# A flamingo block on one core: variance, root and split move to GpSimd, the first norm is joined by bn_aggr, y gets three buffers

## The reference, cut to what matters

```python
x = x + tanh(g_x) * ((ctx @ Wv) @ Wout + bout)         # n_kv == n_q here: one key per query
h = layernorm(layernorm(x), ln1_g, ln1_b)              # width 256
h = bitlinear(h, w1, b1)                               # 1024 wide
h = layernorm(gelu(h), ln2_g, ln2_b)
x = x + tanh(g_f) * bitlinear(h, w2, b2)               # back to 256
# bitlinear: rows scaled by 127 / max|row| and rounded, weights rounded to -1, 0, 1
```

## Time and profile before

| | us |
|---|---|
| median of 3 runs (lowest, highest) | 402.39 (400.57, 402.53) |
| the profiled execution, its own time | 400.17 |
| its span, first to last instruction | 398.4 |
| busy over the span: DVE, PE, ACT, POOL | 330.2, 304.1, 277.9, 220.9 |
| mean granted TensorE clock, share of full | 0.949 |

### The profile page before, as it was taken

How to read it: one execution, slowest core, us unless ns; L and a number is a source line. 1 busy time by engine, 2 the same in 40 slices (tenths; PEclk the granted TensorE clock), 3 DMA queues, 4 the chain that set the end, 5 groups by cost and what they waited for, 6 DMA issues and landing times. The chain is left out here.

```text
span 398.4 us, 5821 instructions
## 1 busy us (share of the span) xinstructions
PE 304.1 (76%) x1690; PEld 187.9 (47%) x1690; DVE 330.2 (83%) x794; ACT 277.9 (70%) x446; POOL 220.9 (55%) x118
## 2 busy tenths in 40 slices
PE   2887295868888888888888888888888766758364
PEld 2776153434646464646464646464646342414043
DVE  0389366888999999999999999999999995957782
ACT  1314447678697979797979797979797968678431
POOL 4021444829484848484848484848485858454600
PEclk9999689989999999999999999999999996969669
DMA  7665404119183828383838383838270707062635
GB/s 226 244 225 181 132 0 130 56 53 185 54 186 107 190 102 182 108 183 110 184 107 184 108 183 109 180 111 172 67 170 18 170 17 160 26 115 71 135 77 160
DMA packets 97686, 51.56 MB, mean 129 GB/s; under 512 B 86535, under 2 KB 88768, under 8 KB 97654
## 3 DMA queue, kind: packets, MB, share of 16 engines
q1 hardware_dynamic: 96758, 51.14, 50.7%
q10 hardware_dynamic: 896, 0.04, 0.1%
HBM read 21.78 MB, written 8.41 MB: 76 GB/s over the span
## 5 line engine op out<-in xcount | busy, mean ns | idle before, releaser
L337 POOL TENSOR_TENSOR y<-u,g_bc 128x1024 f32<-128x1024 f32 x64 | 150.3, 2368 | 62.5 <-DVE parts L594 49.7
L694 DVE TENSOR_TENSOR y<-y,slot_c 128x1024 f32<-128x1024 f32 x64 | 77.7, 1214 | 9.9 <-PE slot_c L965 9.8
L698 DVE TENSOR_REDUCE amax<-y 128x1 f32<-128x1024 f32 x64 | 78.1, 1220 | 2.2
L432 ACT ACTIVATE q<-y,s 128x1024 f16<-128x1024 f32 x64 | 69.8, 1139 | 11.5 <-DVE s L725 11.5
L459 ACT ACTIVATE junk<-u,usum 128x1024 bf16<-128x1024 f32 x64 | 73.5, 1149 | 2.1
L1003 PE MATMUL bank_f<-w2T,q2T 128*128 128x256 f16 x512 | 66.1, 276 | 2.6 <-DVE res L745 2.4
L320 POOL TENSOR_TENSOR rstd<-var,half_neg 128x8 f32<-128x8 f32 x18 | 29.5, 1641 | 69.0 <-DVE var L645 56.6
L965 PE MATMUL slot_c<-ln_rows,rows 128*128 128x512 bf16 x128 | 41.3, 406 | 30.8 <-DVE y L694 16.3
L944 PE MATMUL bank_q<-wvo,ctxT 128*128 128x256 f32 x232 | 59.7, 387 | 0.0
L1003 PEld LDWEIGHTS bank_f<-w2T,q2T 128*128 128x128 f16 x512 | 50.2, 99 | 14.6 <-DVE res L745 4.8
L423 ACT ACTIVATE q<-h,s 128x256 f16<-128x256 f32 x64 | 27.3, 496 | 32.7 <-DVE s L685 32.7
(11 more groups left out here) (114 smaller groups left out, 426.8 us busy)
## 6 DMA issues: line engine op xcount, KB each, us to landing
c_in<-in_ctx SPq DMA_DIRECT2D x16, 512.0 KB, 3.4
x_in<-in_x SPq DMA_DIRECT2D x16, 512.0 KB, 4.1
out<-res SPq DMA_DIRECT2D x32, 256.0 KB, 2.8
y<-in_L_ffn_w SPq DMA_DIRECT2D x2, 1024.0 KB, 9.3
u<-in_L_xattn_Wkv SPq DMA_DIRECT2D x1, 1024.0 KB, 6.8
u<-in_L_xattn_Wout SPq DMA_DIRECT2D x1, 1024.0 KB, 10.0
q2T<-q SPq DMA_TRANSPOSE x64, 3.3
g_bc<-in_L_ffn_ln_g SPq DMA_DIRECT2D x1, 512.0 KB, 4.5
```

The costliest lines, as they stand in the source:

```text
L337: nc.gpsimd.tensor_tensor(y[:, k % 2, t, :], u[:, t, :], g2_bc[:, :], ALU.mult).then_inc(gain2_done, 1)
L432: nc.scalar.activation(q2[:, t, :], y[:, k % 2, t, :], ACT.Copy, scale=s2[:, t:t + 1]).then_inc(q2_done, 1)
L694: nc.vector.tensor_tensor(line, line, slot_c[:, :], ALU.add).then_inc(y_done, 1)
L698: nc.vector.tensor_reduce(amax2[:, t:t + 1], y[:, k % 2, t, :], AX.X, ALU.max, apply_absolute_value=True).then_inc(amax2_done, 1)
```

## The change: what it does

`variance`, `deviations` and `split` run on POOL, as does the new `norm_first`, which turns the first norm's mean and variance into the statistics' form. On DVE four `bn_aggr` replace the seven instructions of `join`, and stand behind the first `row`. `first` and `second` become one `scales` of six instructions over both norms at once. y has three buffers, `rows` two. From stage 3 on attention goes to `slot_a` after its last gelu, both halves at the end of PE's body. `quantise` of t = 2 and 3 moves behind the squares, its transposes (`turn_second`) to the next body of SP, behind a store, and its second product to the next body of PE, between corrections. There is one body more (S + 2). ACT takes the rows ahead of the quantising.

The diff, cut to its core (the renamed buffers and their indices are left out):

```diff
             for i in bodies:
+                if live(i - 3):
+                    store(i - 3, 0)
+                    turn_second(i - 3, 2)
+                    turn_second(i - 3, 3)
                 if live(i):
                     turn_first(i)
-                if live(i - 2):
-                    for t in range(T):
-                        turn_second(i - 2, t)
-                if live(i - 3):
-                    store(i - 3, 0)
-                    store(i - 3, 1)
                 if live(i + 4) and i + 4 > 1:
                     load_x(i + 4)
                 if live(i + 5) and i + 5 > 1:
                     load_context(i + 5)
-            store(S - 1, 0)
-            store(S - 1, 1)
+                if live(i - 2):
+                    turn_second(i - 2, 0)
+                    turn_second(i - 2, 1)
+                if live(i - 3):
+                    store(i - 3, 1)
...
-                    wait(pool, q2_done, T * (k - 2) + t + 1)
+                    wait(pool, q2_done, T * (k - 3) + t + 1)
                     wait(pool, gelu_done, T * k + t + 1)
-                    nc.gpsimd.tensor_tensor(y[:, k % 2, t, :], u[:, t, :], g2_bc[:, :],
+                    nc.gpsimd.tensor_tensor(y[:, k % 3, t, :], u[:, t, :], g2_bc[:, :],
                                             ALU.mult).then_inc(gain2_done, 1)
...
+                def norm_first(k):
+                    wait(pool, moments_done, k + 1)
+                    wait(pool, std_done, k)
+                    wait(pool, split_steps, split_count(k - 2))
+                    nc.gpsimd.tensor_scalar(stat[:, 0, :], moments[:, :, 0], -1.0, None, ALU.mult)
+                    nc.gpsimd.tensor_scalar(var[:, 0, :], moments[:, :, 1], 1.0 + LN_EPS,
+                                            LN_EPS * LN_EPS, ALU.mult, ALU.add) \
+                        .then_inc(var1_done, 1)
+                def variance(k):
+                    wait(pool, square_done, T * k + T)
+                    wait(pool, std_done, i + 2)
+                    wait(pool, split_steps, split_count(i))
+                    nc.gpsimd.tensor_scalar(stat[:, 2, :], usum[:, :], -1.0 / H, None, ALU.mult)
+                    nc.gpsimd.tensor_scalar(var[:, 1, :], usq[:, :], 1.0 / float(H) ** 3, LN_EPS,
+                                            ALU.mult, ALU.add).then_inc(var2_done, 1)
+                def deviations():
+                    wait(pool, rstd_done, i + 2)
+                    wait(pool, split_steps, split_count(i - 1))
+                    nc.gpsimd.tensor_tensor(stat[:, 1:4:2, :], var[:, :, :], rstd[:, i % 2, :, :],
+                                            ALU.mult).then_inc(std_done, 1)
+                def split(n):
+                    shape = [P, T, KINDS, NPART]
+                    if n == 0:
+                        wait(pool, std_done, min(i + 2, S + 2))
+                        wait(pool, var1_done, min(i + 2, S))
+                        wait(pool, var2_done, min(i, S))
+                        wait(pool, scales_ready, scales_after(i - 1))
+                        wait(pool, rows_done, i + 1)
+                    else:
+                        wait(pool, split_steps, split_count(i - 1) + n)
+                    if n % 2 == 0:
+                        value = (stat_t, rest[:, :, :], rest[:, :, :])[n // 2]
+                        op = nc.gpsimd.tensor_copy(
+                            parts_q[:, :, :, 3 * (n // 2):3 * (n // 2) + 3],
+                            value.unsqueeze(3).to_broadcast(shape))
+                    else:
+                        value = (stat_t, rest[:, :, :])[n // 2]
+                        op = nc.gpsimd.tensor_tensor(rest[:, :, :], value,
+                                                     parts_q[:, :, :, 3 * (n // 2)], ALU.subtract)
+                    op.then_inc(split_steps, 1)
                 if -1 <= i <= S:
-                    wait(pool, split_steps, split_count(i))
+                    deviations()
+                if -1 <= i <= S + 1:
+                    for n in range(5):
...
+                    norm_first(0)
+                if i == -1:
+                    norm_first(1)
                 if i == 0:
                     pool.wait_ge(g2_in, 16)
                 if live(i - 1):
-                    if i > 1:
-                        gain(i - 1, 2)
                     gain(i - 1, 3)
                 if live(i + 1) and i > -1:
                     gain_first(i + 1)
+                if live(i + 2) and i > 0:
+                    norm_first(i + 2)
                 if live(i):
                     gain(i, 0)
                     gain(i, 1)
+                    gain(i, 2)
                 if i == 0:
-                    gain(0, 2)
+                    norm_first(2)
+                if live(i):
+                    variance(i)
                 if -1 <= i + 1 <= S:
                     root(i + 1)
...
-                    wait(act, second_ready, second_count(k, t // 2))
+                    wait(act, scales_ready, k + 3 + (t // 2 if k == S - 1 else 0))
                     wait(act, q2T_in[t], 16 * k)
-                    nc.scalar.activation(q2[:, t, :], y[:, k % 2, t, :], ACT.Copy,
-                                         scale=s2[:, t:t + 1]).then_inc(q2_done, 1)
+                    nc.scalar.activation(q2[:, t, :], y[:, k % 3, t, :], ACT.Copy,
+                                         scale=scale[:, (k + 1) % 2, 1, t:t + 1]).then_inc(q2_done, 1)
                 def take_rows():
                     wait(act, rows_done, i + 2)
-                    wait(act, shift1_done, min(i + 1, S))
-                    wait(act, corr_done, T * (i - 1))
-                    wait(act, hid_done, T * min(i, S))
-                    wait(act, ffn_done, T * (i - 2))
-                    nc.scalar.copy(rows[:, :, :].rearrange("p a n -> p (a n)"),
+                    wait(act, shift1_done, min(i, S))
+                    wait(act, corr_done, T * (i - 2))
+                    wait(act, hid_done, T * (i - 1))
+                    wait(act, ffn_done, T * (i - 3))
+                    nc.scalar.copy(rows[:, i % 2, :, :].rearrange("p a n -> p (a n)"),
                                    slot_c[:, 0:P].bitcast(BF16)).then_inc(rows_copied, 1)
...
+                if 0 < i <= S:
+                    take_rows()
+                if live(i + 3) and i > 0:
+                    take_context(i + 3, 0)
                 if live(i - 2):
                     quantise(i - 2, 0)
                     quantise(i - 2, 1)
-                if 0 < i <= S:
-                    take_rows()
+                if live(i + 3) and i > 0:
+                    take_context(i + 3, 1)
+                if live(i):
+                    for t in range(T):
+                        gelu(t)
+                        square(t)
                 if live(i - 2):
                     quantise(i - 2, 2)
                     quantise(i - 2, 3)
                 if i == S + 1:
                     take_rows()
-                if live(i):
-                    gelu(0)
-                    square(0)
-                if live(i + 3) and i > 0:
-                    take_context(i + 3, 0)
-                if live(i):
-                    gelu(1)
-                    square(1)
-                    gelu(2)
-                    square(2)
                 if i == 0:
                     take_context(3, 0)
-                if live(i):
-                    gelu(3)
-                    square(3)
-                if live(i + 3) and i > -3:
-                    take_context(i + 3, 1)
+                    take_context(3, 1)
...
+                def join(k):
+                    wait(dve, bn_done, k + 1)
+                    wait(dve, var1_done, k)
+                    for t in range(T):
+                        op = nc.vector.bn_aggr(moments[:, t, :], bn[:, t, :])
+                    op.then_inc(moments_done, 1)
...
+                def scales(kinds=slice(0, 2), those=slice(0, T)):
+                    shape = [P, kinds.stop - kinds.start, those.stop - those.start]
+                    base = 3 * (i + 1 + (those.start > 0))
+                    one = (slice(None), kinds, those)
+                    power = rstd[:, i % 2, kinds, those]
+                    if kinds.start == 0:
+                        wait(dve, amax1_done, i + 2)
+                    wait(dve, amax2_done, T * (i - 1) + those.stop)
+                    wait(dve, rstd_done, i + 2)
                     wait(dve, split_steps, split_count(i))
-                    nc.vector.tensor_scalar(stat[:, 2, :], usum[:, :], -1.0 / H, None, ALU.mult)
-                    nc.vector.tensor_scalar(var[:, 1, :], usq[:, :], 1.0 / float(H) ** 3, LN_EPS,
-                                            ALU.mult, ALU.add).then_inc(var2_done, 1)
+                    nc.vector.tensor_tensor(amax_g[one], amax[one], power, ALU.mult) \
+                        .then_inc(scale_steps, 1)
+                    wait(dve, scale_steps, base + 1)
```

(86 more changed lines are left out.)

263 lines of the change are left out of this document (60 added, 203 removed).

## The result

The changed kernel takes 416.65 us (median of 4 runs, 412.95 to 417.02) against 402.31 before, a ratio of 1.035 [1.028, 1.041]: 3.5% slower. The prediction of 400.3 (388 to 412) was wrong in sign and outside its range. The profiled execution took 416.72 with a span of 414.9, against 398.4, at a mean granted clock of 0.890 against 0.949.

What follows compares the result with a forecast made beforehand. DVE was taken to set the pace at 19.98 us a stage, the square-to-rows loop binding nearly together. Head 105.2 + stages 249.9 + 1.0 + tail 40.4 gave a 396.5 span, forecast as 400.3 us (388 to 412).

Steps and rivals of the forecast that it cites:

- The loop of a steady stage: From one last square through POOL's splits, rows, corrections and gelus to the next: A + 15.2 = 19.22 us against 19.98.
- A: Time from the last square to the last split, on POOL after the change: 4.0 us against 5.27, bounds 3.3 and 5.9.
- The joining, held at 0.40: Four bn_aggr on DVE between row 0 and row 1, taken to add 0.40 us to the row-to-row 2.40.
- rival 1: POOL's small operations dearer, each 0.1 costing 0.8 a stage: break-even at A = 4.15, 0.5% slower from 4.3; chance 0.27.
- Thirteen stages 249.9, plus 1.0: Stages 2 to 15: 13 x 19.22 us, plus 1.0 of the 3.1 that late stages cost extra.
- both are moved out: PE's attention and ACT's quantising no longer delay correction 0 after the splits: 4.0 to 4.8, where today takes 1.56.
- Head: I take 0: Up to stage 2's last square: no net change, bounds -2 and +3, that square ending at 105.2 us.
- Tail: From stage 15's last square to the end: 40.4 us against 30.3, SP's order holding the transposes; 10.1 more, bounds 6 and 12.
- Rival 2: Engines hold each other: POOL's gain stops bn_aggr (421 us) or its power stops DVE's scales (405.5); chance 0.08.
- two-input rule of the Trainium skill: DVE instructions with two SBUF inputs contend with GpSimd reading SBUF: scales would wait the power's 1.64, giving 405.5; bn_aggr free.
- The 2.12 of the earlier trace: Stall of a 4-element DVE operation, 56.34 to 58.46, beside a POOL gain; taken as the kind the two-input rule describes.
- Rival 3: Faster: A is 3.3 and joining 0.3, stage 18.4, near DVE's own 18.1; time 390, or 386 with tail 36; chance 0.22.

Runs made afterwards that it cites:

- f3_extra: e2_fill with two unused, dependent POOL copies of eight elements a partition between root and deviations: 417.44 us, 1.039 of the kernel before.
- e2_fill: The changed kernel with six idle matmuls on PE ahead of turn_rows in bodies 1 to 16: 408.32 us, 1.020 of the kernel before.
- e1_tail: The changed kernel with SP's order altered in its last two bodies, second transposes ahead of stores: 406.06 us, 1.015 of the kernel before.
- e3_head: The changed kernel with norm_first(0) and body -1's deviations and splits back on DVE: 411.26 us, 1.026 of the kernel before.
- f1_all: The changed kernel with the edits of e1_tail, e2_fill and e3_head together: 398.20 us, 0.991 of the kernel before.

## Why the prediction was wrong

**The loop of a steady stage: right, by misses that cancel, which is luck.** In us from the last square, forecast and measured: splits end 4.0 and 4.39, row 0 5.44 and 5.84, row 1 8.24 and 8.37, correction 2 9.59 and 9.73, gelu 2 14.24 and 14.36, last square 19.22 and 19.21. A was 0.39 too short: the five splits took 1.75 for 1.6, the two operations of the variance 0.48 for 0.35, the gaps around them and the power the rest. The joining, held at 0.40, displaces 0.13 (row to row 2.53 against 2.40), and gelu 2 to the last square takes 4.85 for 4.98. By rival 1's rule an A of 4.39 is a kernel slower by over 0.5%; the stage didn't follow it only because of the other two misses. The kernel was slower, but not by rival 1's mechanism. The rule's slope is right: f3_extra found 0.50 a stage for 0.50 on the line.

**"Thirteen stages 249.9, plus 1.0": wrong, +9.2.** The step that failed: the sum carries every PE term over at its price at full clock (correction and hidden 1.73, a second product 0.99) to all thirteen stages, and puts the clock at nothing, without a reason. I wrote "both are moved out" of attention and the quantising, and counted it as a gain; PE's pause in front of turn_rows was what that left. In nine of the thirteen stages the clock fell and second products took up to 1.9; e2_fill shows the cause by filling the pause, and is within 0.3 of the forecast.

**"Head: I take 0": wrong, +6.9**, over the bound of +3. With the same head e1_tail is 3.5 over, so up to half of the miss is scatter. I weighed POOL holding DVE and never the reverse. In the head the first norm's small operations lie beside DVE's rounding of the weights; e3_head is 6.0 earlier at the root after stage 0. The Trainium skill (SBUF — State Buffer, Who interferes with whom) says that DVE's `tensor_scalar` can run in a two-port mode and then holds the pair of ports it shares with GpSimd for the whole instruction. The trace agrees: 1.26 for an operation of 0.19, ended 0.06 behind DVE's. By the roots of after, 3.8 of the miss stand at the end of stage 0, 3.8 in stage 1 (22.45 for 18.64), and stage 2 gives back 0.5. For stage 1 I had named 2.2, for both context copies behind all squares and attention behind them, and set it off against a gain of 1.3 in stage 2. With this code stage 1 was 1.15 over before's in e1_tail, at full clock, and 3.8 over in after, at a clock of 0.88: the low clock goes with the larger part, but no run separates it.

**Tail: the mechanism right, the size 2.4 short.** From the last square, forecast and measured: transposes of (14, 2) issued 20.4 and 20.2; quantising of (15, 3) ends 26.3 and 26.1; finals of stage 14 end 27.3 and 28.3; last transposes issued from 31.1 and at 31.9; last final ends 37.9 and 40.3. Twice two second products of 1.75 to 1.91 at the lower clock stand where I had 1.04. e1_tail took 10.0 off by the order on SP, close to the 10.1 of the forecast; in f1_all it was 6.

**Rival 2** (stalls of DVE beside POOL): no bn_aggr went over 0.18, and in the steady stage the scales' products beside the power took 0.14 to 0.17 (151.27 to 151.63, power from 151.19). In body 0 one product (L693) took 2.21 beside a gain, once in the run. The two-input rule of the Trainium skill that the prediction weighed, from the same section, would stop such a product beside any POOL instruction that reads SBUF. The traces agree for a gain (2.21 here, 2.08 for a product of 0.16 at 61.58 in before) and not for the power, in both kernels. The 2.12 of the earlier trace rows, which the prediction counted for this rule, was a `tensor_scalar` with one tensor as input, so it is no case of two inputs. **Rival 3** needed an A of 3.3. (19.98 less 1.8 is 18.2, not the prediction's 18.1; nothing hangs on it.)

## What to carry to other kernels

When work moves away from in front of a wait of PE, look at what PE does in that wait before and after: a shorter loop with one concentrated pause ran 6% slower in most stages than the same loop with idle matmuls in it. Look at each new neighbour in the prologue and the drain as well as in the steady stage; here they cost 6.9 and 12.5 us in the profiles, against the 2.8 that the thirteen stages gave. Small operations in a dependent line are worth moving one by one to an engine that idles beside them: one of 0.22 gave 0.24 a stage.

## What the runs showed of the hardware

- Clock: the granted level fell behind PE's pause ahead of turn_rows in 9 of after's 13 stages; with six idle matmuls in that pause it fell in none of e2_fill's ten middle ones. PE's busy time over 200 us was higher after (176.2) than before (169.6), whose clock stayed at full. Part of that is the lower clock itself, but a stage of after at full clock (131.99 to 151.19) has 16.65 of 19.20, 0.87, and one of before (145.66 to 165.65) 17.07 of 19.99, 0.85: the mean busy time did not tell which kernel keeps its clock.
- POOL on 4 to 24 elements a partition: 0.19 to 0.27, a copy 0.22, a broadcast cast 0.29, with 0.06 to 0.08 between dependent ones and 0.14 ahead of the power (1.67).
- DVE: bn_aggr 0.15 each and 0.37 for four; behind a long operation four cost 0.14.
- DVE and POOL: small POOL operations of 0.19 and 0.25 took 1.26 and 1.10 beside DVE's `tensor_scalar` on 2048 elements; DVE's small products took 2.08 and 2.21 beside a POOL gain, and 0.12 to 0.17 beside the power.
